# Neighbour attention over 25,000 edges: the node products of blocks 0 to 13 kept in PSUM

## The chip, the cores and the metric

One core of a Trainium2 chip. The time is the device time of one execution in microseconds; of several executions the median is given. A second number, the span, goes from the first to the last instruction of one profiled execution.

## The reference

50,000 nodes with 64 features, 25,000 edges sorted by destination, 10 relations. Each edge's source and destination row is multiplied with its relation's 64x64 matrix, a score comes from both and the edge's features, a softmax over the edges of one destination weighs the source rows, and the sum updates the node. A layer norm over all nodes follows.

```python
proj = jnp.einsum('ni,rio->nro', nfeat, relation_weight)
t_r = proj[src, etype]
h_r = proj[dst, etype]
att = jnp.sum(t_r * jnp.tanh(h_r + efeat), axis=-1)
ex = jnp.exp(att - segment_max(att, dst)[dst])
a = ex / segment_sum(ex, dst)[dst]
h_nb = jax.ops.segment_sum(nfeat[src] * a[:, None], dst, num_segments=n)
out = leaky_relu((nfeat + h_nb) @ res_fc_w.T, 0.01) + leaky_relu(nfeat * h_nb @ res_fc2_w.T, 0.01)
x = _layernorm(x + out, axis=-1)
```

A node without edges has h_nb = 0, so its row needs x and one product alone.

## The kernel before

**Two kinds of work.** The dense part runs over all nodes in 49 tiles of 1,024 rows (128 x 512 numbers): transposes on TensorE into `tr_ps`, a copy to `dT` on ScalarE, a product with `bd_cat` into `y_ps`, relu and sum into `zd`, mean and variance, scaling into `o_t`, store. The edge part runs over 25 blocks of 8 columns of 128 edges (the last block has 4). A partition holds consecutive edges, so a segment's sums run along its columns. GpSimd gathers the source and the destination row of each column with one indirect DMA a column and side into `xsd` (L450, 388 of them; four columns come in single rows over SyncE's queue) and later scatters the finished rows with one indirect DMA a column (L474, 196), which overwrite the dense rows of the nodes with edges. All gathers stand ahead of all scatters in GpSimd's list.

**Steps.** Every engine runs a list in a fixed order, step by step, s from -1 to 28. In step s the edge part projects block s, takes scores, weights and sums of block e = s-1, ends block f = s-2 (node products), centres block l = s-3 and scales an earlier one (`final_out`, from step 5 on). Up to step 15 it also takes the dense tiles D0, D1, D2 = 3s+3, 3s+4, 3s+5 (step 15 has one). For the projection VectorE makes nine masked copies `xm` of the transposed rows (`mask`, L999, a ring of four) and TensorE multiplies each, and one plain copy `xc`, with a relation's matrix (`quad`, ten a step, L558 and L560).

**The pair.** For a block that ends, ScalarE scales the sums into h (`heads`, L779), VectorE makes uw = (h + x, h * x) (`pair`, L1092 and L1093), TensorE transposes it into `tr_ps` in two groups (`pair_turn`, L588), ScalarE copies each to `uwT` (`pair_copy`, L788) and TensorE multiplies with the weights.

- Blocks 0 to 13 (f < LATE = 14): h is in SBUF (`h_t`). Four quarters of the product go one after the other into a half of `s_ps` (`pair_y`, L598) and are copied to `l12` in SBUF (`pair_out`, L793). VectorE takes leaky relu over l12 (`leaky`, L1099), adds its halves (`final_add`, L1104) and x (`final_add_x`, L1109).
- Blocks 14 to 24, when no dense tile is left that uses `y_ps`: h is in `y_ps`. The products with `bd_relu` (0.99 of the weights) go to `y_ps` (L609), the linear part (0.01 of the weights, `bd_lin`) to `tr_ps` (L616). VectorE adds relu of both and the linear part to x straight from PSUM (L1114, L1119, L1125).

Three groups of users share PSUM: `tr_ps` the dense transposes and the pair's, `y_ps` the dense tiles (until step 15), `s_ps` scores and quarters.

**GpSimd's waits.** Ahead of each gather or scatter `pace` may wait for TensorE: a list of marks, made by `pe_marks`, gives TensorE's work in instructions (16 a quad, 16 a dense product, 8 for four transposes), and transfer n waits for the last mark at or below n x 14.6 - 250 (13.64 for a scatter). A gather of block s also waits for the end of block s-13, a scatter for `final_out` of its block. Between the scatters of blocks 20 and 21 GpSimd gathers `es_end`, from which the last node of each partition is mended at the end.

## Time and profile before

| | us |
|---|---|
| median of 3 runs | 761.22 (760.61 to 765.5) |
| the profiled execution | 762.27 |
| its span | 760.5 |
| mean granted clock of TensorE in it | 0.921 of 2.4 GHz |

Durations and starts below come from the profiled execution, counted from the start of its span. The profile lists each engine's busy time, groups of instructions by line, what ended an engine's idle time, and the granted clock by stretch (1.00 is 2.4 GHz, 0.50 is 1.2 GHz). Handing over a DMA is not counted as busy, so GpSimd's time between two indirect DMAs appears as idle time put down to "issue".

### The profile page before, as it was taken

What the parts mean: (1) busy time and instruction counts of PE and PEld (TensorE: products, weight loads), DVE (VectorE), ACT (ScalarE), POOL (GpSimd) and SP (SyncE); (2) the same over time, 40 slices, a digit from 0 to 9 for tenths busy, and PEclk for the clock granted to TensorE, in tenths of its full rate; (3) what the DMA queues carried; (4) which work ended last, traced back from release to release, by engine and by line L of the source; (5) the groups of instructions that cost most, each with busy time, mean ns of one, the idle gap of its engine ahead of it and who ended that gap; (6) DMA issues with size and microseconds to landing.
All of it is one profiled execution on the core that took longest, in us unless ns stands there. A gap on an engine that the chain in (4) does not pass through costs nothing. (4 is left out here: it accounts for less than half of the span.)

```text
span 760.5 us, 13886 instructions
## 1 busy us (share of the span) xinstructions
PE 574.4 (76%) x3948; PEld 313.6 (41%) x3948; DVE 603.9 (79%) x1094; ACT 507.9 (67%) x1457; POOL 575.6 (76%) x594
## 2 busy tenths in 40 slices
PE   1897988888898898798898797898888988650000
PEld 0643454444454454454454453444444444450000
DVE  2589899999999999999999999899888888750010
ACT  0376877779879878878878879656655556770040
POOL 6777777777777777777777777777777777777776
PEclk9999999999999999999999999999999999855555
DMA  4643443343353343354343243321222210000000
GB/s 115 177 123 91 137 152 114 97 151 85 108 165 107 94 155 92 113 151 109 93 155 108 67 124 97 105 67 48 75 75 73 68 48 33 32 25 18 19 18 16
DMA packets 48034, 70.37 MB, mean 93 GB/s; under 512 B 15970, under 2 KB 19486, under 8 KB 47958
## 3 DMA queue, kind: packets, MB, share of 16 engines
q1 hardware_dynamic: 18562, 32.97, 13.8%
q0 software_dynamic: 18752, 17.29, 10.5%
q10 hardware_dynamic: 10644, 19.23, 6.8%
q8 instruction: 32, 0.52, 0.3%
q14 instruction: 44, 0.36, 0.2%
HBM read 45.60 MB, written 25.78 MB: 94 GB/s over the span
## 5 line engine op out<-in xcount | busy, mean ns | idle before, releaser
L450 POOL DMA_INDIRECT xsd<-in_x,ends_i x388 | 380.8, 982 | 119.9 <-issue 107.7
L999 DVE SCALAR_TENSOR_TENSOR xm<-typ,xT_ps 128x1024 f32<-128x1024 f32 (+1 forms) x225 | 264.2, 1184 | 3.0 <-ACT xc L719 2.6
L558 PE MATMUL t_ps<-xm,w_rel 64*64 64x512 f32 (+1 forms) x900 | 241.5, 617 | 13.7 <-DVE xm L999 11.0
L560 PE MATMUL h_ps<-xm,w_rel 64*64 64x512 f32 (+1 forms) x900 | 241.4, 617 | 0.0
L474 POOL DMA_INDIRECT out<-out_r,row_i x196 | 191.7, 978 | 59.7 <-issue 57.0
L578 PE MATMUL y_ps<-bd_cat,dT 128*128 128x256 f32 x392 | 98.4, 395 | 11.3 <-DVE zd L1061 5.4
L743 ACT ACTIVATE o_t<-zd,rstd 128x64 f32<-128x64 f32 x392 | 98.8, 339 | 6.3 <-DVE rstd L1083 6.3
L558 PEld LDWEIGHTS t_ps<-xm,w_rel 64*64 64x64 f32 x900 | 46.9, 133 | 105.2 <-DVE xm L999 76.8
L578 PEld LDWEIGHTS y_ps<-bd_cat,dT 128*128 128x128 f32 x392 | 72.7, 196 | 25.1 <-ACT dT L724 11.0
L588 PE MATMUL tr_ps<-ident,uw 128*128 128x128 f32 x196 | 33.5, 297 | 44.5 <-ACT uwT L788 24.0
L1041 DVE SCALAR_TENSOR_TENSOR es<-es,wd,wx 128x64 f32<-128x64 f32 x196 | 55.2, 282 | 11.2 <-DVE es L1041 0.5
L598 PEld LDWEIGHTS s_ps<-bd_both,uwT 128*128 128x128 f32 x224 | 31.9, 206 | 59.7 <-issue 38.6
L588 PEld LDWEIGHTS tr_ps<-ident,uw 128*128 128x128 f32 x196 | 21.6, 146 | 84.1 <-issue 52.7
L767 ACT ACTIVATE wx<-xsd,wd 128x64 f32<-128x64 f32 x196 | 52.1, 337 | 0.8
L598 PE MATMUL s_ps<-bd_both,uwT 128*128 128x128 f32 x224 | 42.6, 316 | 8.8 <-issue 8.7
L813 ACT ACTIVATE out_r<-zcf,rstd 128x64 f32<-128x64 f32 x196 | 49.1, 333 | 0.0
L1061 DVE TENSOR_TENSOR zd<-rd,y_ps 128x512 f32<-128x512 f32 x49 | 33.3, 680 | 19.1 <-ACT rd L729 17.9
L560 PEld LDWEIGHTS h_ps<-xm,w_rel 64*64 64x64 f32 x900 | 46.9, 133 | 0.0
L761 ACT ACTIVATE wd<-delta 128x16 f32<-128x16 f32 (+1 forms) x25 | 5.4, 216 | 61.6 <-DVE delta L1029 55.6
L806 ACT ACTIVATE sqf<-zcf 128x512 f32<-128x512 f32 (+1 forms) x25 | 15.3, 611 | 43.4 <-DVE zcf L1136 42.2
L736 ACT ACTIVATE sqd<-zd 128x512 f32<-128x512 f32 x49 | 30.9, 630 | 19.8 <-DVE zd L1071 12.0
L713 ACT ACTIVATE g_t<-h_ps 128x512 f32<-128x512 f32 (+1 forms) x25 | 14.7, 588 | 39.1 <-PEq L563 38.3
(161 smaller groups left out, 957.9 us busy)
## 6 DMA issues: line engine op xcount, KB each, us to landing
x_in<-in_x SPq DMA_DIRECT2D x48, 256.0 KB, 2.7
typ<-typ_d SPq DMA_DIRECT2D x24, 512.0 KB
out<-o_t ACTq DMA_DIRECT2D x48, 256.0 KB
xsd<-in_x SPq DMA_DIRECT2D x512, 0.2 KB
xsd<-in_x,ends_i POOLq DMA_INDIRECT x388, 2.7
hist<-es ACTq DMA_DIRECT2D x24, 256.0 KB, 2.7
ea<-in_edge_attr SPq DMA_DIRECT2D x24, 224.0 KB
out<-out_r,row_i POOLq DMA_INDIRECT x196, 2.1
```

The costliest lines, as they stand in the source:

```text
L450: pool.indirect_dma_start(xsd[:, s % RX, j, side, :], None, x[:, :], bass.IndirectOffsetOnAxis(ap=ends_i[:, side, c:c + 1], axis=0),).then ...
L474: pool.indirect_dma_start(out[:, :], bass.IndirectOffsetOnAxis(ap=row_i[:, c:c + 1], axis=0), out_r[:, s % RW, j, :], None, bounds_check=t ...
L558: pe.matmul(t_ps[h * D:(h + 1) * D, 0:n], w[0:D, :], moving[0:D, h * n:(h + 1) * n], start=(at == 0), stop=(at == R - 1), skip_group_check ...
L560: mm = pe.matmul(h_ps[(1 - h) * D:(2 - h) * D, 0:n], w[D:P, :], moving[D:P, (1 - h) * n:(2 - h) * n], start=False, stop=(at == R - 1), ski ...
L578: mm = pe.matmul(y_ps[:, j * 2 * P:(j + 1) * 2 * P], dT[:, d % 2, j * P:(j + 1) * P], bd_cat.rearrange("p k f -> p (k f)"), start=True, st ...
L588: mm = pe.transpose(tr_ps[:, j * P:(j + 1) * P], uw[:, g * QUAD + j, :, :].rearrange("p k f -> p (k f)"), ident[:, :])
L598: mm = pe.matmul(s_ps[:, YQ + j * P:YQ + (j + 1) * P], uwT[:, q // 2, k * P:(k + 1) * P], bd_both[:, :], start=True, stop=True)
L743: ins = act.activation(o_t[:, d % RO, j * D:(j + 1) * D], zd[:, d % RZ, j * D:(j + 1) * D], ACT.Copy, scale=rstd[:, s % 2, d % 3, j:j + 1])
L767: ins = act.activation(wx[:, j, :], xsd[:, e % RX, j, 0, :], ACT.Copy, scale=wd[:, e % 2, 0, j:j + 1])
L813: ins = act.activation(out_r[:, f % RW, j, :], zcf[:, f % 2, j, :], ACT.Copy, scale=rstd[:, s % 2, 3, j:j + 1])
L999: v.scalar_tensor_tensor(xm[:, m % RM, 0:n], typ[:, s % RT, 0:n], float(r), xT_ps[:, 0:n], ALU.is_equal, ALU.mult).then_inc(masked, 1)
L1041: v.scalar_tensor_tensor(es[:, e % RS, j, :], old, wd[:, e % 2, 1, j:j + 1], wx[:, j, :], ALU.mult, ALU.add).then_inc(chain_done, 1)
```

## The change

All blocks take one form. h goes to `tr_ps` (`heads_ps`); the eight products with `bd_relu` go to `y_ps` between the dense tiles D0 and D1 (`pair_y`), the linear part to `s_ps` (`pair_linear`), which the scores use too; VectorE reads h, the products and the linear part from PSUM. `h_t`, `l12`, `pair_out` and `leaky` go. The order moves with it. TensorE: D1's transposes before the products; D2's transposes behind quad 8; quad 9 before D2's product. ScalarE: `tanh` from the step's start to its end; `weights` behind `dense_square`; the pair's copies before and between the `weigh`s, ahead of `final_out`. VectorE: the two relu sums behind mask 6, the linear part behind D1's sum, `final_centre` before mask 6. New waits: `dense_y(D1)` for `relu_second`, `pair_y` for D0's sum, `scores` and `pair_linear` for earlier linear sums, `pair_copy` for all products of the block before. GpSimd's own list and its constants stay; the marks that it waits for are listed in the new order.

```diff
...
@@ -84,7 +83,6 @@
     def quad_count(m):
         return m // RB * R + m % RB + (2 if m % RB >= PLAIN_AT else 1)
-    LATE = (ND - 1) // 3 - 2
     ROW_BLOCKS = [8, 13, 19, 24]
     CHUNK = 16
...
-        def h_late():
-            return y_ps[:, 0:COLS * D].rearrange("p (j f) -> p j f", f=D)
-        def y_late(k, n):
+        heads_ps = tr_ps.rearrange("p (j f) -> p j f", f=D)
+        def y_pair(k, n):
             return y_ps.rearrange("p (j k f) -> p j k f", j=COLS, k=2)[:, 0:n, k, :]
-        def lin_late(n):
-            return tr_ps[:, 0:n * D].rearrange("p (j f) -> p j f", f=D)
+        def y_lin(n):
+            return s_ps[:, 0:n * D].rearrange("p (j f) -> p j f", f=D)
         def turn(n, ring):
             return n // ring + 1
...
@@ -285,24 +275,24 @@
                     mark(att_done, e + 1, 2 * cols(e))
                 multiplied(0)
                 quads(0, 4)
-                if quarters > 0:
+                if pairs:
                     mark(tr_in, TR_PAIR[f, 0] + 1, 8)
                 quads(4, 5)
-                if quarters > 2:
+                if pairs > 1:
                     mark(tr_in, TR_PAIR[f, 1] + 1, 8)
                 quads(5, 6)
-                paired(0)
                 turned(1)
+                if pairs:
+                    mark(y12_done, 2 * f + 1, 2 * cols(f))
                 quads(6, 7)
-                paired(1)
                 multiplied(1)
                 quads(7, 8)
-                paired(2)
+                if pairs:
+                    mark(y12_done, 2 * f + 2, 2 * cols(f))
+                quads(8, 9)
                 turned(2)
-                quads(8, 9)
-                paired(3)
+                quads(9, 10)
                 multiplied(2)
...
                 pe.wait_ge(prod_done, e + 1)
-                wait(pe, delta_done, e)
-                if e >= 2:
-                    pe.wait_ge(pf_done, Q_BEFORE[min(e - 1, LATE)])
+                wait(pe, z2_done, e - 1)
                 half = cols(e) // 2
-                b = (e % 2) * COLS
                 for i in range(half):
-                    pe.matmul(s_ps[:, b + 2 * i:b + 2 * i + 2], prod[:, i * P:(i + 1) * P], ones2[:, :],
+                    pe.matmul(s_ps[:, 2 * i:2 * i + 2], prod[:, i * P:(i + 1) * P], ones2[:, :],
                                    start=True, stop=True)
...
@@ -574,6 +561,8 @@
             def dense_y(d):
                 pe.wait_ge(tr_out, TR_DENSE[d] + 1)
                 wait(pe, zadd_done, d)
+                if d % 3 == 1:
+                    wait(pe, z1_done, d // 3 - 2)
                 for j in range(4):
                     mm = pe.matmul(y_ps[:, j * 2 * P:(j + 1) * 2 * P], dT[:, d % 2, j * P:(j + 1) * P],
                                    bd_cat.rearrange("p k f -> p (k f)"), start=True, stop=True)
...
-            def pair_y(f, q):
-                pe.wait_ge(tr_out, TR_PAIR[f, q // 2] + 1)
-                wait(pe, pf_done, Q_BEFORE[f] + q)
-                wait(pe, delta_done, min(f + 2, NS))
-                for j in range(2):
-                    k = (q % 2) * 2 + j
-                    mm = pe.matmul(s_ps[:, YQ + j * P:YQ + (j + 1) * P], uwT[:, q // 2, k * P:(k + 1) * P], bd_both[:, :],
-                                   start=True, stop=True)
-                mm.then_inc(y12_done, 1)
-            def late_y(f, g):
-                pe.wait_ge(tr_out, TR_PAIR[f, g] + 1)
-                pe.wait_ge(uw_done, f + 1)
-                if f > LATE:
-                    pe.wait_ge(z1_done, f)
-                for k in range(QUAD):
-                    j = g * QUAD + k
+            def pair_y(f):
+                pe.wait_ge(tr_out, TR_PAIR[f, groups(f) - 1] + 1)
+                pe.wait_ge(zadd_done, min(ND, 3 * f + 10))
+                wait(pe, z1_done, f)
+                for j in range(cols(f)):
+                    g, k = divmod(j, QUAD)
                     mm = pe.matmul(y_ps[:, j * P:(j + 1) * P], uwT[:, g, k * P:(k + 1) * P], bd_relu[:, :], start=True, stop=True)
                 mm.then_inc(y12_done, 1)
-            def late_linear(f, g):
-                pe.wait_ge(tr_out, TR_PAIR[f, groups(f) - 1] + 1)
-                for k in range(QUAD):
-                    j = g * QUAD + k
-                    mm = pe.matmul(tr_ps[:, j * D:(j + 1) * D], uwT[:, g, k * P:(k + 1) * P], bd_lin[:, :], start=True, stop=True)
+            def pair_linear(f):
+                pe.wait_ge(delta_done, min(f + 2, NS))
+                wait(pe, z2_done, f)
+                for j in range(cols(f)):
+                    g, k = divmod(j, QUAD)
+                    mm = pe.matmul(s_ps[:, j * D:(j + 1) * D], uwT[:, g, k * P:(k + 1) * P], bd_lin[:, :], start=True, stop=True)
                 mm.then_inc(y12_done, 1)
-            def pair_part(f, q):
-                if f < LATE:
-                    pair_y(f, q)
-                elif q < groups(f):
-                    late_y(f, q)
-                else:
-                    late_linear(f, q - groups(f))
...
                 if main:
                     quad(s, 5)
-                if quarters > 0:
-                    pair_part(f, 0)
                 if D1 is not None:
                     dense_turn(D1)
+                if ending:
+                    pair_y(f)
                 if main:
                     quad(s, 6)
-                if quarters > 1:
-                    pair_part(f, 1)
                 if D1 is not None:
                     dense_y(D1)
                 if main:
                     quad(s, 7)
-                if quarters > 2:
-                    pair_part(f, 2)
-                if D2 is not None:
-                    dense_turn(D2)
+                if ending:
+                    pair_linear(f)
                 if main:
                     quad(s, 8)
                 if s == NS:
...
                 if D2 is not None:
+                    dense_turn(D2)
+                if main:
+                    quad(s, 9)
+                if D2 is not None:
                     dense_y(D2)
...
                 act.wait_ge(frec_done, f + 1)
-                wait(act, uw_done, f)
-                if f == LATE:
-                    act.wait_ge(zadd_done, ND)
-                if f > LATE:
-                    act.wait_ge(z1_done, f)
-                h = h_late() if f >= LATE else h_t
+                wait(act, tr_out, TR_PAIR[f, 0])
                 for j in range(g * QUAD, (g + 1) * QUAD):
-                    ins = act.activation(h[:, j, :], es[:, f % RS, j, :], ACT.Copy, scale=rs[:, f % 2, j:j + 1])
+                    ins = act.activation(heads_ps[:, j, :], es[:, f % RS, j, :], ACT.Copy, scale=rs[:, f % 2, j:j + 1])
                 ins.then_inc(h_done, 1)
             def pair_copy(f, g):
                 act.wait_ge(tr_in, TR_PAIR[f, g] + 1)
-                if f > LATE:
-                    act.wait_ge(y12_done, Q_BEFORE[f])
-                elif f > 0:
-                    act.wait_ge(y12_done, min(Q_BEFORE[f - 1] + 2 * g + 2, Q_BEFORE[f]))
+                wait(act, y12_done, 2 * f)
                 act.copy(uwT[:, g, :], tr_ps[:, :]).then_inc(tr_out, 1)
-            def pair_out(f, q):
-                act.wait_ge(y12_done, Q_BEFORE[f] + q + 1)
-                wait(act, z1_done, f)
-                act.copy(l12[:, 2 * q:2 * q + 2, :, :],
-                         s_ps[:, YQ:YQ + 2 * P].rearrange("p (j k f) -> p j k f", j=2, k=2)).then_inc(pf_done, 1)
             def roots(s):
...
                 D0, D1, D2 = (n if n in tiles(s) else None for n in (3 * s + 3, 3 * s + 4, 3 * s + 5))
                 DP = 3 * s + 2 if 3 * s + 2 in tiles(s - 1) else None
-                quarters, done = 2 * groups(f) if 0 <= f < NS else 0, tiles(s - 1)
-                if 0 <= e < NS:
-                    tanh(e)
...
                     store_o(n)
-                if 0 <= s - 2 < NS:
-                    store_hist(s - 2)
-                if 0 <= e < NS:
-                    weights(e)
-                    weigh(e, 0)
+                if ending:
+                    store_hist(f)
                 if DP is not None:
                     dense_square(DP)
+                if on:
+                    weights(e)
+                if ending:
+                    pair_copy(f, 0)
+                if on:
+                    weigh(e, 0)
+                if ending and groups(f) > 1:
+                    pair_copy(f, 1)
+                if on and groups(e) > 1:
+                    weigh(e, 1)
                 if 0 <= o - 1 < NS and s <= NS:
                     final_out(o - 1, s - 1)
-                if quarters > 0:
-                    pair_copy(f, 0)
-                if 0 <= e < NS and groups(e) > 1:
-                    weigh(e, 1)
-                if quarters > 2:
-                    pair_copy(f, 1)
                 if s >= 0:
                     roots(s)
-                if quarters > 0 and f < LATE:
-                    pair_out(f, 0)
                 if D1 is not None:
                     dense_copy(D1)
...
                     final_square(l)
-                if D1 is not None:
-                    dense_relu(D1)
-                if quarters > 2 and f < LATE:
-                    pair_out(f, 2)
+                for n in done[1:2]:
+                    dense_norm(n)
+                for n in done[1:2]:
+                    store_o(n)
                 if D2 is not None:
                     dense_copy(D2)
-                for n in done[1:2]:
-                    dense_norm(n)
-                if quarters > 3 and f < LATE:
-                    pair_out(f, 3)
-                for n in done[1:2]:
-                    store_o(n)
+                if 0 <= s < NS:
+                    tanh(s)
                 if D1 is not None:
...
                     v.wait_ge(tr_in, TR_PAIR[f - 1, groups(f - 1) - 1] + 1)
-                h = h_late() if f >= LATE else h_t
-                v.tensor_tensor(uw[:, 0:n, 0, :], h[:, 0:n, :], xd, ALU.add)
-                v.tensor_tensor(uw[:, 0:n, 1, :], h[:, 0:n, :], xd, ALU.mult).then_inc(uw_done, 1)
-            def leaky(f):
+                v.tensor_tensor(uw[:, 0:n, 0, :], heads_ps[:, 0:n, :], xd, ALU.add)
+                v.tensor_tensor(uw[:, 0:n, 1, :], heads_ps[:, 0:n, :], xd, ALU.mult).then_inc(uw_done, 1)
+            def relu_first(f):
                 n = cols(f)
-                v.wait_ge(pf_done, Q_BEFORE[f + 1])
-                l = l12[:, 0:n, :, :].rearrange("p j k f -> p (j k f)")
-                v.scalar_tensor_tensor(l, l, SLOPE, l, ALU.mult, ALU.max).then_inc(l_done, 1)
-            def final_add(f):
+                wait(v, fsub_done, f)
+                v.wait_ge(y12_done, 2 * f + 1)
+                v.scalar_tensor_tensor(zf[:, 0:n, :], y_pair(0, n), 0.0, xsd[:, f % RX, 0:n, 1, :], ALU.max, ALU.add).then_inc(l_done, 1)
+            def relu_second(f):
                 n = cols(f)
                 v.wait_ge(l_done, f + 1)
-                v.tensor_tensor(zf[:, 0:n, :], l12[:, 0:n, 0, :], l12[:, 0:n, 1, :], ALU.add).then_inc(z1_done, 1)
-            def final_add_x(f):
+                v.scalar_tensor_tensor(zf[:, 0:n, :], y_pair(1, n), 0.0, zf[:, 0:n, :], ALU.max, ALU.add).then_inc(z1_done, 1)
+            def linear_last(f):
                 n = cols(f)
                 v.wait_ge(z1_done, f + 1)
-                v.tensor_tensor(zf[:, 0:n, :], zf[:, 0:n, :], xsd[:, f % RX, 0:n, 1, :], ALU.add).then_inc(z2_done, 1)
-            def late_first(f):
-                n = cols(f)
-                v.wait_ge(y12_done, Q_BEFORE[f] + groups(f))
-                v.scalar_tensor_tensor(zf[:, 0:n, :], y_late(0, n), 0.0, xsd[:, f % RX, 0:n, 1, :], ALU.max, ALU.add).then_inc(l_done, 1)
-            def late_second(f):
-                n = cols(f)
-                v.wait_ge(l_done, f + 1)
-                v.scalar_tensor_tensor(zf[:, 0:n, :], y_late(1, n), 0.0, zf[:, 0:n, :], ALU.max, ALU.add).then_inc(z1_done, 1)
-            def late_third(f):
-                n = cols(f)
-                v.wait_ge(z1_done, f + 1)
-                v.wait_ge(y12_done, Q_BEFORE[f + 1])
-                v.tensor_tensor(zf[:, 0:n, :], zf[:, 0:n, :], lin_late(n), ALU.add).then_inc(z2_done, 1)
+                v.wait_ge(y12_done, 2 * f + 2)
+                v.tensor_tensor(zf[:, 0:n, :], zf[:, 0:n, :], y_lin(n), ALU.add).then_inc(z2_done, 1)
             def final_sum(f):
                 n = cols(f)
...
                 if late:
                     final_sum(l)
+                if late:
+                    final_centre(l)
                 if main:
                     mask(s, 6)
+                if ending:
+                    relu_first(f)
+                if ending:
+                    relu_second(f)
                 if on:
                     sum_one(e, 4)
                     sum_one(e, 5)
...
                 if D0 is not None:
                     dense_centre(D0)
-                if late:
-                    final_centre(l)
...
                 if D1 is not None:
                     dense_add(D1)
+                if ending:
+                    linear_last(f)
                 if D1 is not None:
...
                     inverse(e)
-                if ending and f < LATE:
-                    leaky(f)
-                    final_add(f)
-                if ending and f >= LATE:
-                    late_first(f)
-                    late_second(f)
                 if main:
                     product(s)
-                if ending and f < LATE:
-                    final_add_x(f)
-                if ending and f >= LATE:
-                    late_third(f)
                 if D0 is not None:
                     dense_sum(D0)
...
```

## Rows read from the trace of the kernel before

**Rows 1.** the page's first part: busy time of each engine, its share of the span, instructions

```profile
PE 574.4 (76%) x3948; PEld 313.6 (41%) x3948; DVE 603.9 (79%) x1094; ACT 507.9 (67%) x1457; POOL 575.6 (76%) x594
```

**Rows 2.** the chain that ended last, its last scatter: start, us, what

```profile
754.85 0.97 POOL out L474
```

**Rows 3.** GpSimd's gathers by line: shortest/median/longest ns, first and last start

```profile
L450 POOL DMA_INDIRECT xsd<-in_x,ends_i x388: 938/944/1660, 3.5 to 502.2; - x194
```

**Rows 4.** timeline of VectorE at the end: start, us, what [idle before it, releaser]

```profile
721.17 0.28 DVE L1274 SCALAR_TENSOR_TENSOR before<-es_end,fix,xT_ps 128x64 f32<-128x64 f32 x1 [36.89 <-DMA es_end<-hist,fix_i]
```

**Rows 5.** gathers by stretch (33:88, 88:469, 479:503): busy us, mean ns | idle, releasers

```profile
L450 POOL DMA_INDIRECT xsd<-in_x,ends_i x44 | 42.3, 961 | 14.1 <-issue 12.2 <-PE y_ps L578 0.7 <-PE h_ps L560 0.6
...
L450 POOL DMA_INDIRECT xsd<-in_x,ends_i x296 | 292.1, 987 | 90.3 <-issue 82.4 <-PE h_ps L560 6.4 <-PE s_ps L598 0.9
...
L450 POOL DMA_INDIRECT xsd<-in_x,ends_i x20 | 18.9, 947 | 6.1 <-issue 5.5 <-PE h_ps L560 0.6
```

**Rows 6.** timeline of GpSimd in step 9

```profile
284.10 1.29 POOL L450 DMA_INDIRECT xsd<-in_x,ends_i  x1 [0.30 <-PE h_ps L560]
...
301.97 1.65 POOL L450 DMA_INDIRECT xsd<-in_x,ends_i  x1 [0.31 <-issue]
```

**Rows 7.** timeline of VectorE in step 9

```profile
279.00 1.21 DVE L999 SCALAR_TENSOR_TENSOR xm<-typ,xT_ps 128x1024 f32<-128x1024 f32 x1
...
284.49 0.68 DVE L1093 TENSOR_TENSOR uw<-h_t,xsd 128x512 f32<-128x512 f32 x1
...
301.57 1.23 DVE L1099 SCALAR_TENSOR_TENSOR l<-l 128x1024 f32<-128x1024 f32 x1
302.83 0.69 DVE L1104 TENSOR_TENSOR zf<-l 128x512 f32<-128x512 f32 x1
...
304.48 0.68 DVE L1109 TENSOR_TENSOR zf<-zf,xsd 128x512 f32<-128x512 f32 x1
```

**Rows 8.** timeline of VectorE in a step of the late form

```profile
511.18 0.64 DVE L1114 SCALAR_TENSOR_TENSOR zf<-y_ps,xsd 128x512 f32<-128x512 f32 x1
511.85 0.69 DVE L1119 SCALAR_TENSOR_TENSOR zf<-y_ps,zf 128x512 f32<-128x512 f32 x1
```

**Rows 9.** steps: length; busy of PE, PEld, DVE, ACT, POOL; clock, DMA

```profile
142.80:170.10 27.30, 24.07 (x167) 13.14 (x167) 26.50 (x47) 21.86 (x63) 20.90 (x22) 1.00 0.41 123
...
198.70:227.30 28.60, 25.29 (x168) 13.71 (x169) 26.67 (x46) 24.00 (x72) 21.85 (x22) 0.94 0.42 124
227.30:255.40 28.10, 23.73 (x168) 13.07 (x168) 26.57 (x46) 23.80 (x71) 21.46 (x22) 1.00 0.40 119
```

**Rows 10.** timeline of ScalarE in step 9

```profile
285.80 0.63 ACT L736 ACTIVATE sqd<-zd 128x512 f32<-128x512 f32 x1 [0.49 <-DVE zd L1071]
286.34 2.00 ACT L813 ACTIVATE out_r<-zcf,rstd 128x64 f32<-128x64 f32 x8
...
293.60 0.35 ACT L793 COPY l<-s_ps 128x256 f32<-128x256 f32 x1
293.85 0.59 ACT L724 COPY dT<-tr_ps 128x512 f32<-128x512 f32 x1
...
304.57 1.01 ACT L719 COPY xc<-xT_ps 128x1024 f32<-128x1024 f32 x1 [0.74 <-PEq L522]
```

**Rows 11.** timeline of TensorE in step 9 and in a late step

```profile
288.96 0.96 PE L588 MATMUL tr_ps<-ident,uw 128*128 128x128 f32 x4 [2.06 <-ACT uwT L788]
...
294.75 1.89 PE L578 MATMUL y_ps<-bd_cat,dT 128*128 128x256 f32 x8
...
303.45 1.06 PE L520 MATMUL xT_ps<-ident,xsd 128*128 128x128 f32 x8 [0.30 <-issue]
...
509.29 1.10 PE L616 MATMUL tr_ps<-bd_lin,uwT 128*128 128x64 f32 x8
```

**Rows 12.** timeline of TensorE: last matmuls of block 5's second quad

```profile
168.02 0.59 PE L558 MATMUL t_ps<-xm,w_rel 64*64 64x512 f32 x1
```

**Rows 13.** timeline of GpSimd: the gather that asks for it

```profile
177.42 0.94 POOL L450 DMA_INDIRECT xsd<-in_x,ends_i  x1 [0.30 <-issue]
```

37 lines of the change are left out of this document (11 added, 26 removed).

## The prediction

> **What bounds the kernel.** I read the engines' sums on the page first. No engine looks full: VectorE 79%, TensorE and GpSimd 76%, ScalarE 67% [rows 1]. The chain that ended last says more: it consists of GpSimd's scatters alone, one after the other, 0.97 us each, the last at 754.85 [rows 2]. So I read GpSimd's own instructions next. The 388 gathers start at 3.5 us and have a median of 944 ns [rows 3]; the idle time before one is 90.3/296 = 0.305 us and is almost all put down to "issue", the handing over of a DMA [rows 5]. The 584 transfers at 0.944 or 0.97 plus 0.305 make 388 x 1.249 + 196 x 1.275 = 735 of the 751 us from the first start to the last: they stand back to back, and the 16 us left are a few at the start and gathers longer than the median. GpSimd's 76% is a full engine. At the end compute waits for it, too: VectorE stood still for 36.89 us before L1274 until GpSimd's gather of es_end had landed [rows 4]. The kernel ends when GpSimd has issued its list, provided compute never makes it wait. What the change does to VectorE, ScalarE and TensorE counts only through two doors: whether a gather gets longer or shorter, and whether the waits of `pace` or `fmul_done` begin to hold GpSimd.
>
> **First door: lengthened gathers.** The median is 944 ns, the mean is not. From 88 to 469 us there are 296 gathers with a mean of 987; from 33 to 88, before any block ends, 961; from 479 on 947 [rows 5]. The timeline of one step (9) shows where it comes from. The gather at 284.10 took 1.29 us and ended at 285.39; VectorE ran the two instructions of `pair` (uw from h_t and xsd, all in SBUF) to 285.17. The gather at 301.97 took 1.65 us and ended at 303.62; VectorE ran L1099 and L1104 (l12 and zf, all in SBUF) to 303.52. Neighbouring gathers have 0.94 [rows 6, 7]. Such a pair of long gathers recurs in nearly every step that ends one of blocks 0 to 13. In the late steps, where the same work reads PSUM (L1114, L1119, L1125), the gathers stay near 947 [rows 5, 8]. The change gives blocks 0 to 13 exactly the late form: h, both products and the linear part are read from PSUM, so each of these VectorE instructions keeps one SBUF input. What the gain is: at least 987 - 961 = 26 ns, at most 987 - 947 = 40 ns a gather, over 296 gathers 7.7 to 11.8 us. I take the middle, 9.7, because the dense tiles' L1071 (two SBUF inputs, three a step) stays and is in the 961, while the late steps lack it.
>
> The Trainium skill, "SBUF — State Buffer", section "Who interferes with whom", has this mechanism: a VectorE instruction with two SBUF inputs contends with a GpSimd instruction that reads SBUF, and one with at most one such input does not. It also infers that `tensor_tensor` does not hold up descriptor generation, which would speak against the gain (761 by that); the ends of the two gathers above, 0.10 to 0.22 us after the VectorE instruction, disagree.
>
> **VectorE.** Removed a block: L1099 (1.23), L1104 (0.69), L1109 (0.68), 2.60 us. Added: 0.64 + 0.69 and, for L1125's sum of the same 128 x 512, 0.68 again, 2.01 [rows 7, 8]. That is 0.6 us less in a step; a step without final_out takes 27.30 with VectorE busy for 26.50 [rows 9]. **ScalarE** loses four `pair_out` copies (0.36 each, about 0.25 from start to start: L793 at 293.60, L724 at 293.85), 1.0 to 1.4 us [rows 10]. **TensorE** gets more: eight bd_relu products cost what eight bd_both cost, and the eight bd_lin ones are new. The late steps show 1.10 for four, so 2.2 us a step [rows 11]. None of these sets the end, so none is added to the time; they decide the length c of a compute step.
>
> **Second door: pace.** `pace` asks, before gather n, that TensorE has passed a mark of n x 14.6 - 250 in its list. A full dense step weighs 328 in it (24+16+16+48+160+16+32+16; the changed list gives 328 as well), so GpSimd takes 328/14.6 = 22.47 gathers a step. Before, one took (292.1+90.3)/296 = 1.292 us, 29.0 a step, against compute's 28.1 to 28.6 [rows 5, 9]. Gather 134 (the first is 0), the 135th, starts at 177.42 and asks for 1,706, that is block 5's second quad, done at 168.6: TensorE leads by 8.8 us there [rows 12, 13]. After the change a gather takes 1.292 - 9.7/296 = 1.259 us, so a step of GpSimd is 28.3 us. The lead at step 5 is 8.8, less 83 x 0.033 = 2.7, plus about 1.2 for three compute steps 0.4 shorter: 7.3. Over the ten full steps 5 to 14 GpSimd is held for 10 x (c - 28.3) - 7.3, if that is positive.
>
> **The length of a step.** Count from the step's first mask, T. Before, in step 9 (T = 279.00), ScalarE reached `dense_square` of the last tile at T+6.8, and TensorE stood 2.06 us at the second transpose of the pair for uwT, because final_out (2.0 us) ran before the copy. Table loads and roots ended at T+14.6, the copy dT at T+15.4, and TensorE went on to D1's product with no pause, at T+15.75 [rows 7, 10, 11]. After, the square, both copies, both weighs, final_out and the roots all still stand ahead of that copy; weights and the first weigh (1.3 us) come behind the square instead of before it, a wait of about 0.4 for TensorE's transposes is added, and the first pair_out (0.25) and the 0.18 wait of the second copy go: T+15.4 + 1.3 + 0.4 - 0.4 = T+16.7. TensorE, rid of the 2.06 but a little later at the start, has done pair_y and quad 6 by about T+14.1 and now waits some 2.5 us there, before dense_y(D1). The pause has moved, not gone. From D1's product to the end of the next plain copy took 304.57 + 1.01 - 294.75 = 10.8 before [rows 10, 11]; the linear part adds 2.2 and the two quarters that stood there take 1.1 away: 11.9. So c = 16.7 + 11.9 = 28.6, with the overlap of the next mask 28.5, at full clock. VectorE has 27.3 - 0.6 = 26.7 of work and waits about 0.6 for the first wx, 0.7 for the linear part, 0.4 for tanh: 28.4. Both agree.
>
> The clock is the unknown. Of the ten steps from 170 to 454 six show a granted clock of 0.94 (2.4 GHz, but 1.2 for a part), with TensorE busy for 25.29 instead of 23.73; all came behind pauses of 2.06 us, and the step went from 28.1 to 28.6 [rows 9, 11]. After, what follows the pause sets the step, so a fall costs between 0.5 and 1.56. I take 1.0, six times in ten: c = 29.1. GpSimd is then held for 8 - 7.3 = 0.7 us, say 1.4 for uneven steps. Bounds: c = 28.5 gives none, c = 30.1 gives 10.7.
>
> **Other parts.** New waits: `dense_y(D1)` waits for `relu_second`, which VectorE finishes near T+16.3, just ahead of the copy above; if late by x, quad 7 and everything behind it on TensorE is late by x. `scores` waits for the z2 of two blocks earlier, done a step before. D2's x load is released one or two quads later and has a ring of four tiles. z2 comes earlier, so GpSimd's ring wait only eases. Scatters: compute waits 36.89 us for es_end before its last blocks, so an end that comes 10 us sooner leaves it 27 [rows 4].
>
> **Sum.** The profiled execution took 762.3 us, 760.5 of it the span; its time is 1.1 above the median of the three runs. 762.3 - 9.7 + 1.4 = 754.0 for it, and 1.1 less, 752.9, for the median: 753.0.
>
> **Rivals.** (A) Forecast: gathers shrink, pace holds GpSimd under 2 us: 749.5 to 753.6. Chance 0.46. (B) The gathers shrink, but the pause with its clock fall makes c 29.4 to 30.4: held 4 to 14 us, 755 to 765; at c = 29.7, 758. For it: the lead is only 7.3. Chance 0.30. (C) The gathers don't shrink, since other VectorE instructions with two SBUF inputs (L1071, L1136, L1041) catch them now that their phase is free: 761. Against it: the 961 of the early steps. Chance 0.10. (D) Slower: TensorE becomes the bound. Every step has the fall at full price (28.5 + 1.56) and dense_y(D1) waits 0.7 more for `relu_second`: c = 30.8, held 25 - 7.3 = 17.7, 769. It decides from c = 30.0 on, where held time exceeds the 9.7 gained. Chance 0.14.
>
> **Numbers.** About 1% (7.6 us) is what can be told from no change. Faster by more is A, 0.46; within it B and C, 0.40; slower D, 0.14. The range of eight in ten is 749 to 765; A's own is 749.5 to 753.6.
>
> **What will show it.** The mean gather from 88 to 469 us (987, expected 955), no gather of 1.65 us, idle before gathers beyond 0.31 us put down to TensorE (expected under 2 us in all), wx-to-wx steps near 29, TensorE's pause before L578 instead of L588, and the granted clock there. Wrong would be the prediction above all if that pause grew beyond 3 us, or if gathers lengthen at L1071.

## The result, and the profile after

| | before | after |
|---|---|---|
| median of 22 runs each, us | 761.72 | 766.44 |
| ratio, 95% interval | | 1.005, 1.0038 to 1.0062 |
| the profiled execution: time, span | 762.3, 760.5 | 768.5, 766.7 |
| GpSimd's 388 gathers: busy, idle before | 380.8, 119.9 | 373.6, 130.8 |
| first scatter at | 503.4 | 508.9 |

The change is 0.5% slower, within the 1% that the forecast called no change, and outside its range of 749 to 765. First the sums of the page after, to be held against [rows 1], and its two groups of indirect DMAs (busy us, mean ns | idle before, its main releaser):

```profile
PE 595.8 (78%) x4172; PEld 346.9 (45%) x4172; DVE 602.6 (79%) x1094; ACT 496.3 (65%) x1401; POOL 569.1 (74%) x594
...
L440 POOL DMA_INDIRECT xsd<-in_x,ends_i x388 | 373.6, 963 | 130.8 <-issue 102.0
...
L464 POOL DMA_INDIRECT out<-out_r,row_i x196 | 192.4, 982 | 61.5 <-issue 54.8
```

The gathers did get shorter, by 7.2 us, and the idle time before them grew by 10.9 us, which is no longer all "issue". The rest of the 6.2 us of span is 0.7 in the scatters' own time and 1.8 in the idle time before them. From 88 to 469 us, as [rows 5]:

```profile
L440 POOL DMA_INDIRECT xsd<-in_x,ends_i x293 | 282.5, 964 | 99.3 <-issue 77.3 <-PE h_ps L547 8.6 <-PE y_ps L567 5.6
```

The mean fell from 987 to 964 ns, and TensorE's lines now hold gathers: `pace` has begun to wait. Four steps of the kernel after (3, 4, 8 and 9; length, busy time and count of PE, PEld, DVE, ACT, POOL, granted clock, DMA share), as [rows 9]:

```profile
109.50:138.90 29.40, 25.87 (x175) 15.53 (x175) 26.32 (x47) 20.35 (x59) 22.18 (x24) 0.94 0.41 116
138.90:168.70 29.80, 26.51 (x183) 15.80 (x182) 26.53 (x47) 21.15 (x60) 21.24 (x22) 0.94 0.40 114
...
256.90:285.30 28.40, 24.88 (x182) 15.25 (x182) 26.43 (x46) 23.09 (x68) 21.46 (x22) 1.00 0.41 119
285.30:315.30 30.00, 26.52 (x182) 15.67 (x182) 26.37 (x46) 23.07 (x68) 22.05 (x23) 0.94 0.39 115
```

A step takes 28.4 us with the clock at 2.4 GHz all along and 30.0 where it is at 1.2 GHz for a part; before it took 28.1 and 28.6. Steps 3 and 4 took 27.3 before and now have a fall each. Their pause ahead of D1's product ends with `relu_second` (L1045) and not with the copy, here in step 3:

```profile
124.57 0.69 DVE L1045 SCALAR_TENSOR_TENSOR zf<-y_ps,zf 128x512 f32<-128x512 f32 x1
125.41 3.65 PE L567 MATMUL y_ps<-bd_cat,dT 128*128 128x256 f32 x8 [2.73 <-DVE zf L1045]
```

In step 9 (T = 285.33), the rows round D1's product:

```profile
300.82 0.69 DVE L1045 SCALAR_TENSOR_TENSOR zf<-y_ps,zf 128x512 f32<-128x512 f32 x1
301.28 0.57 ACT L689 COPY dT<-tr_ps 128x512 f32<-128x512 f32 x1
301.90 2.76 PE L567 MATMUL y_ps<-bd_cat,dT 128*128 128x256 f32 x8 [2.76 <-ACT dT L689]
...
306.48 2.00 PE L593 MATMUL s_ps<-bd_lin,uwT 128*128 128x64 f32 x16
308.58 0.69 DVE L1051 TENSOR_TENSOR zf<-zf,s_ps 128x512 f32<-128x512 f32 x1 [1.86 <-PE s_ps L593]
308.75 0.94 POOL L440 DMA_INDIRECT xsd<-in_x,ends_i  x1 [0.53 <-PE s_ps L593]
```

TensorE stands 2.76 us for the copy `dT` of D1. `relu_second` (L1045), its second gate, ended only 0.34 us before the copy did (301.51 and 301.85). The fall of the clock comes behind: D1's product takes 2.76 instead of 1.9 us. `pair_linear` follows late, VectorE waits 1.86 us for it, and so does a gather. One wait at the end is new as well, the first scatter's, for the last dense store. That store is issued at 505.81; before, it was at 489.05, 14 us ahead of the first scatter at 503.42. Now:

```profile
508.90 1.00 POOL L464 DMA_INDIRECT out<-out_r,row_i  x1 [2.08 <-DMA out<-o_t]
```

### The profile page after: what moved, and what is told of

Its sections match the earlier page's. It is cut to its first block and busy times, and to the rows that moved or that the text cites. A ratio compares the mean times of both kernels' runs of the same rounds, so it can differ in the third digit from the quotient of the medians.

```text
span 766.7 us, 14235 instructions
## 1 busy us (share of the span) xinstructions
PE 595.8 (78%) x4172; PEld 346.9 (45%) x4172; DVE 602.6 (79%) x1094; ACT 496.3 (65%) x1401; POOL 569.1 (74%) x594
## 5 line engine op out<-in xcount | busy, mean ns | idle before, releaser
L440 POOL DMA_INDIRECT xsd<-in_x,ends_i x388 | 373.6, 963 | 130.8 <-issue 102.0
L943 DVE SCALAR_TENSOR_TENSOR xm<-typ,xT_ps 128x1024 f32<-128x1024 f32 (+1 forms) x225 | 264.5, 1185 | 7.7 <-ACT xc L684 7.5
L545 PE MATMUL t_ps<-xm,w_rel 64*64 64x512 f32 (+1 forms) x900 | 234.9, 617 | 29.4 <-DVE xm L943 28.8
L567 PE MATMUL y_ps<-bd_cat,dT 128*128 128x256 f32 x392 | 111.1, 433 | 48.5 <-ACT dT L689 35.0
L708 ACT ACTIVATE o_t<-zd,rstd 128x64 f32<-128x64 f32 x392 | 98.5, 335 | 16.3 <-DVE rstd L1025 16.3
L593 PEld LDWEIGHTS s_ps<-bd_lin,uwT 128*128 128x128 f32 x392 | 47.8, 199 | 22.0 <-issue 22.0
L585 PE MATMUL y_ps<-bd_relu,uwT 128*128 128x128 f32 x392 | 51.5, 287 | 1.5 <-ACT uwT L745 1.4
L585 PEld LDWEIGHTS y_ps<-bd_relu,uwT 128*128 128x128 f32 x392 | 48.0, 200 | 10.0 <-ACT uwT L745 10.0
L593 PE MATMUL s_ps<-bd_lin,uwT 128*128 128x64 f32 x392 | 51.1, 286 | 0.0
L739 ACT ACTIVATE tr_ps<-es,rs 128x64 f32<-128x64 f32 x196 | 48.6, 302 | 1.3
L694 ACT ACTIVATE rd<-y_ps 128x512 f32<-128x512 f32 x49 | 28.7, 585 | 25.9 <-PE y_ps L567 25.9
L745 ACT COPY uwT<-tr_ps 128x512 f32<-128x512 f32 x49 | 28.6, 584 | 25.5 <-PE tr_ps L575 24.2
```

Of the source, the lines that this page charges most:

```text
L440: pool.indirect_dma_start(xsd[:, s % RX, j, side, :], None, x[:, :], bass.IndirectOffsetOnAxis(ap=ends_i[:, side, c:c + 1], axis=0),).then ...
L545: pe.matmul(t_ps[h * D:(h + 1) * D, 0:n], w[0:D, :], moving[0:D, h * n:(h + 1) * n], start=(at == 0), stop=(at == R - 1), skip_group_check ...
L567: mm = pe.matmul(y_ps[:, j * 2 * P:(j + 1) * 2 * P], dT[:, d % 2, j * P:(j + 1) * P], bd_cat.rearrange("p k f -> p (k f)"), start=True, st ...
L585: mm = pe.matmul(y_ps[:, j * P:(j + 1) * P], uwT[:, g, k * P:(k + 1) * P], bd_relu[:, :], start=True, stop=True)
L593: mm = pe.matmul(s_ps[:, j * D:(j + 1) * D], uwT[:, g, k * P:(k + 1) * P], bd_lin[:, :], start=True, stop=True)
L708: ins = act.activation(o_t[:, d % RO, j * D:(j + 1) * D], zd[:, d % RZ, j * D:(j + 1) * D], ACT.Copy, scale=rstd[:, s % 2, d % 3, j:j + 1])
```

## The experiments

**Which chip.** The first four runs and the last two were taken where the kernel before takes 762 to 763 us. The others fell where it takes 911 to 927; they are compared only with the kernel before beside them and have a section of their own.

In the expectations, **theory P:** the pause ahead of D1's product, with the fall behind it, gives GpSimd's gain back through `pace`. **Rival V:** VectorE's order of masks and relus sets the step, and the pause only shows it. **Rival L:** the gathers stay long, since other instructions with two SBUF inputs hold them.

### Is it the lead? LEAD 600 in both kernels

```diff
-PACE, LEAD, PACE_OUT = 14.6, 250, 13.64
+PACE, LEAD, PACE_OUT = 14.6, 600, 13.64
```

In the kernel after:

> The changed kernel with LEAD 600 in place of 250, so that pace asks some 24 gathers later; compute is untouched. Theory P: the compute step stays 28.4 to 30, but GpSimd is held later or not at all: 10 to 12 us fewer, 754 to 757, unless another wait of GpSimd comes in the place of pace. Rival C (compute itself ends late, pace only shows it): 764 to 767, with GpSimd's waits now put down to o_stored, z2 or fmul.

766.16 us, 1.0063 [1.0043, 1.0083]. The groups of the page, and the wait ahead of the first scatter in the timeline:

```profile
L440 POOL DMA_INDIRECT xsd<-in_x,ends_i x388 | 371.5, 957 | 119.1 <-issue 108.8
...
505.50 1.00 POOL L464 DMA_INDIRECT out<-out_r,row_i  x1 [12.54 <-DMA out<-o_t]
```

No gather is held any more: 11.7 us of idle time are gone and the gathers are 9.3 us shorter than before. Nothing of it reaches the end. GpSimd arrives sooner and stands 12.54 us for the last store of `o_t`, since the scatters overwrite dense rows. Compute's dense phase is a second wall at 505.5, and `pace` only spreads the same wait over the gathers. So this run's rival C is borne out: the loss isn't a matter of pacing, the dense steps are too long.

In the kernel before:

> The kernel before with LEAD 600. Its gathers have an idle time of 0.305 us whatever they wait for, but for two early waits of 0.3 and 0.4 us. Theory P: 760 to 761.5, no difference. Rival: earlier gathers crowd the DMA queues or meet VectorE elsewhere: over 763 or under 758.

762.7 us, 1.0004 [0.9988, 1.002], idle before gathers 119.1 against 119.9. Before, `pace` held next to nothing.

### Are the gathers held by what the forecast said? h in PSUM alone

The kernel before with h of blocks 0 to 13 in `tr_ps`:

```diff
-                h = h_late() if f >= LATE else h_t
+                h = h_late() if f >= LATE else lin_late(COLS)
```

> The kernel before with one part of the change alone: in blocks 0 to 13 the scaled sums h go to tr_ps, which is free there, in place of h_t in SBUF, so that both instructions of pair keep one SBUF input. Nothing else moves. Theory G (a gather is held until a VectorE instruction with two SBUF inputs ends, and its own end comes 0.82 us later): the gathers held by pair, 10 to 14 of them with 3.3 to 5.4 us in all, go, those held by leaky stay: 756 to 759. Rival N (the lengthening has another cause than the inputs' place): 761 to 762.

761.6 us, 0.9992 [0.9979, 1.0005]: theory G's 756 to 759 didn't come. The gathers' busy time fell by 1.3 us only, 380.8 to 379.5, and that isn't clear of chance (383.1 in the kernel before with LEAD 600). The timeline of the same place in its step 9 says why:

```profile
283.80 0.68 DVE L1094 TENSOR_TENSOR uw<-tr_ps,xsd 128x512 f32<-128x512 f32 x1
284.01 0.94 POOL L450 DMA_INDIRECT xsd<-in_x,ends_i  x1 [0.30 <-issue]
284.40 0.68 DVE L1095 TENSOR_TENSOR uw<-tr_ps,xsd 128x512 f32<-128x512 f32 x1
284.99 0.68 DVE L1073 SCALAR_TENSOR_TENSOR zd<-zsd,zd 128x512 f32<-128x512 f32 x1
285.25 1.24 POOL L450 DMA_INDIRECT xsd<-in_x,ends_i  x1 [0.30 <-issue]
```

`pair` (L1094 and L1095, now with one input in PSUM) holds nothing: the gather that started 0.21 us into it took 0.94. The next one started 0.26 us into `dense_centre` (L1073 here, L1071 in the kernel before), which has both inputs in SBUF, and ended at 286.49, 0.82 us after that instruction did. That is the rule in all traces. In the kernel before, 49 of the 50 gathers that took over 0.964 us ended 0.81 to 0.82 us after the end of a VectorE instruction with two SBUF inputs that was running as they started; in the kernel after 33 of 34 (0.81 to 0.83). The other one is the very first gather in both. So the forecast named the wrong ends. In [rows 6, 7] the gather at 301.97 ended 0.82 after L1099, not 0.10 after L1104, and the one at 284.10 ended 0.82 after the first instruction of `pair`, not 0.22 after L1093:

```profile
283.88 0.68 DVE L1092 TENSOR_TENSOR uw<-h_t,xsd 128x512 f32<-128x512 f32 x1
```

Taking one such instruction away lets the next one catch a gather. In the kernel after it is `dense_centre` (L1013):

```profile
279.91 0.69 DVE L1013 SCALAR_TENSOR_TENSOR zd<-zsd,zd 128x512 f32<-128x512 f32 x1
280.00 1.42 POOL L440 DMA_INDIRECT xsd<-in_x,ends_i  x1 [0.30 <-issue]
```

### The copy first

The kernel after, `dense_copy(D1)` ahead of `final_out` and the roots:

```diff
+                if D1 is not None:
+                    dense_copy(D1)
                 if 0 <= o - 1 < NS and s <= NS:
                     final_out(o - 1, s - 1)
                 if s >= 0:
                     roots(s)
-                if D1 is not None:
-                    dense_copy(D1)
```

> The changed kernel, with ScalarE's copy of D1 moved ahead of final_out and the roots. Theory P (the pause before D1's product makes the compute step long, with its clock falls; pace passes that on to GpSimd): TensorE's pause of 2.8 us before D1's product goes, no granted clock below 1.00 in steps 5 to 14, a step is 28.1 us or less, GpSimd's idle time over 0.305 a gather falls from about 12 to under 3 us: 753 to 757 us. Rival L (pace's list and lead as such hold GpSimd, whatever ScalarE's order): 765 to 768. Rival M (the pause only moves to another place, as it did with the change): steps stay 28.4 to 30, 763 to 768.

776.54 us, 1.0199 [1.0165, 1.0233]: 10 us worse, where theory P wanted a gain. The timeline of its step 9:

```profile
299.73 0.58 ACT L689 COPY dT<-tr_ps 128x512 f32<-128x512 f32 x1
300.21 2.02 ACT L764 ACTIVATE out_r<-zcf,rstd 128x64 f32<-128x64 f32 x8
302.34 0.69 DVE L1062 SCALAR_TENSOR_TENSOR zcf<-zs,zf 128x512 f32<-128x512 f32 x1 [0.58 <-ACT out_r L764]
304.80 0.69 DVE L1045 SCALAR_TENSOR_TENSOR zf<-y_ps,zf 128x512 f32<-128x512 f32 x1
305.63 0.67 PE L567 MATMUL y_ps<-bd_cat,dT 128*128 128x256 f32 x2 [3.14 <-DVE zf L1045]
```

The copy is early and TensorE waits longer, for the other gate: a later `final_out` delays `final_centre`, which waits for its buffer, which delays the relus behind it. The two gates hang together through ScalarE's list, and theory P, which knew one of them, was too small; a pause that only moves is what its rival M had said.

### Runs on the slower chips

There the compute engines show much more idle time put down to issue, and the mean granted clock is 0.82 to 0.87 instead of 0.92. TensorE's waits in the kernel after (its run beside the third doubled `zf`; waited for, us, times, longest):

```profile
PE y_ps L567 <- issue: 56.0, 30, 7.2
PE t_ps L545 <- issue: 27.3, 18, 4.2
PE y_ps L567 <- DVE zf L1045: 25.8, 8, 7.3
```

A dense step takes 34 to 40 us, `pace` holds GpSimd throughout (247.2 us idle before gathers), and compute is the bound of every kernel. What causes it stays open. It needn't belong to the chip: the record gives number 4 to the chip where the kernel before took 912 and, fifty minutes later, to one where it took 763. The durations of single instructions are as elsewhere (a mask 1,185 ns, a gather 962), so what shows in rows is still to be used. Two kernels tried both gates earlier. First `dense_copy(D1)` between `final_out` and the roots, and, on VectorE, both relus ahead of mask 6 (ScalarE's move is shown):

```diff
-                if s >= 0:
-                    roots(s)
                 if D1 is not None:
                     dense_copy(D1)
+                if s >= 0:
+                    roots(s)
```

> The changed kernel with both gates ahead of D1's product opened a little: ScalarE copies D1 right behind final_out, ahead of the roots, and VectorE runs the two relu sums ahead of mask 6. Theory G2 (two gates stand close behind each other, the copy of D1 at T+16.6 and the relu sums at T+16.2, so that moving one alone gains nothing; the first scatter adds a third wall, the last dense store): the pause before D1's product falls from 2.8 to about 1.5 us, steps to 27.5 to 28.4, GpSimd is held for under 4 us: 756 to 760. Rival M (the pause moves on to another place): 763 to 768.

> The kernel after with dense_copy(D1) between final_out and the roots (the table load and roots, 1.3 us, go behind it) and both relus of the pair ahead of mask 6. Each gate of D1's product comes about 1.2 us sooner, none is put behind final_out. Theory P: pause 1.5 us instead of 2.8, at the price of the roots 0.6 us later; falls of the clock become rare; steps near 28, time 756 to 761. Rival V: the pause goes but mask 6 is later by 1.4 us and quad 6, in front of D1's product, waits for it: the pause moves there and time stays 763 to 768.

1.0283 [1.0214, 1.0351] and, on another chip, 1.0257 [1.0177, 1.0337]. Second, the copy ahead of `final_out`, the relus right behind `final_sum`, and `zf` with two buffers (the moves aren't shown):

```diff
-        zf = sb("zf", [P, COLS, D])
+        zf = sb("zf", [P, 2, COLS, D])
```

> The changed kernel with zf in two buffers, so that the relu sums wait neither for final_centre nor, through it, for final_out; they run before it, and D1's copy runs ahead of final_out and the roots. Theory G2: the pause before D1's product is under 1 us, no clock falls in steps 5 to 14, steps of 26.8 to 28, GpSimd back to back and no wait for the last dense store: 753 to 757, below both kernels. Rival M: steps of 28.4 and more, 763 to 768.

> The kernel after with dense_copy(D1) ahead of final_out and the roots, zf with two buffers and the relus right behind final_sum, and pair_linear where the change put it. Both gates of D1's product (the copy and relu_second) come some 1.5 to 2.5 us sooner. Theory P: the pause shrinks below 1.5 us, most falls of the clock go, steps near 27.8, time 753 to 758. Rival V: final_centre, now behind the relus, waits for a late final_out and delays mask 6 and what follows; steps stay at 29 to 30, 764 to 776.

> dense_copy(D1) ahead of final_out, zf with two buffers, relus right behind final_sum, pair_linear in its place, again. On a chip where the kernel before takes about 762: theory P: pause before D1's product under 1.5 us, most falls of the clock gone, 753 to 758; rival V: 764 to 776, since final_centre waits for a later final_out and delays mask 6. On a chip where the kernel before takes over 900: 4% slower than before, as twice already.

1.0415 [1.0323, 1.0508], 1.0419 [1.0352, 1.0486] and 1.0331 [1.0287, 1.0374]. The kernel after as it is, on the chip of the last of these:

> The kernel after, unchanged, for comparison on the same chip. On a chip where the kernel before takes about 762: 764 to 768. On a chip where the kernel before takes over 900, where compute is the bound: theory P says 2.5 to 3.5% slower than before, since the pause and the 2.2 us of pair_linear behind it count in every step there (the same move of pair_linear was worth 20 us between the two kernels with zf doubled); rival V says at most 1% slower.

1.0132 [1.0086, 1.0178], less than the 2.5 to 3.5% that theory P gave. So the doubled `zf` with its order costs 2 points where compute is the bound: TensorE's wait ahead of D1's product does shrink there, from 3.2 to 1.7 us a step (mean of steps 5 to 14), but the one ahead of D2's grows from 1.2 to 2.1. Neither order was run where the kernel before takes 762, so what they would do there isn't shown.

**The dummy instructions.** The kernel before with 32 VectorE instructions of 128 x 512 more in steps 17 to 24, once with two SBUF inputs, once with one:

```diff
+                if 17 <= s < NS:
+                    v.scalar_tensor_tensor(rd[:, 1, :], rd[:, 0, :], 1.0, sqd[:, 0, :], ALU.mult, ALU.add)
```

```diff
+                if 17 <= s < NS:
+                    v.tensor_reduce(zsd[:, :], rd[:, 0, :].rearrange("p (j f) -> p j f", f=D), AX.X, ALU.add)
```

> The kernel before with four more VectorE instructions in each of the steps 17 to 24 (32 in all), 128 x 512, both inputs in SBUF, 0.69 us; they compute nothing that is used. Theory G: each catches a scatter with a chance of 0.69/1.275 and holds it for 0.35 on average: scatters 4 to 7 us longer in all, 765 to 769. Rival (their VectorE time costs, not their inputs): the same time as its twin with one input. Rival N: 761 to 762.

> The twin: the same 32 places, instructions of 0.68 us with one input in SBUF (a sum along the row). Theory G: no scatter is held by them: 761 to 762, since the late steps have time left (21.2 + 2.7 us against GpSimd's 24). Rival (VectorE's time costs): as its twin, above 764.

913.91 and 911.58 us, against 911.86: the time says nothing, since GpSimd isn't the bound there. The timeline does. With two inputs, then with one:

```profile
654.12 0.68 DVE L1198 SCALAR_TENSOR_TENSOR rd<-rd,sqd 128x512 f32<-128x512 f32 x1
654.25 1.40 POOL L474 DMA_INDIRECT out<-out_r,row_i  x1 [1.29 <-PE h_ps L560]
```

```profile
652.73 0.68 DVE L1198 TENSOR_REDUCE zsd<-rd 128x8 f32<-128x512 f32 x1
652.91 0.97 POOL L474 DMA_INDIRECT out<-out_r,row_i  x1 [1.33 <-PE h_ps L560]
```

All six scatters that started 0.13 to 0.40 us into a dummy with two inputs took 1.14 to 1.40 us and ended 0.84 to 0.85 us after the dummy. The thirteen that started 0.13 to 0.51 us into a dummy with one input took 0.97 to 0.98. The two dummies differ in their operation too, but the kernels' own instructions settle that. Over all twenty traces, 465 transfers started 0.10 us or more into a VectorE instruction with two SBUF inputs and 0.20 or more before its end: every one was held. Of 3,750 that started so in one with an input of two in PSUM (the masks, `pair`, the relus, `scalar_tensor_tensor` and `tensor_tensor` alike) none took over 0.03 us more than usual. It is the number of SBUF inputs, not the work.

### pair_linear in the pause

The kernel after with its eight products, ready since `pair_copy`, ahead of `dense_y(D1)`; the mark that `pace` reads moves along:

```diff
+                if ending:
+                    pair_linear(f)
                 if D1 is not None:
                     dense_y(D1)
                 if main:
                     quad(s, 7)
-                if ending:
-                    pair_linear(f)
```

> The kernel after with one move in TensorE's list: pair_linear (eight products, 2.2 us, whose operands have been ready since pair_copy) goes ahead of dense_y(D1), into the pause; the mark that pace reads moves with it. Theory P (the 2.8 us pause before D1's product and what stands behind it set the step, at 28.4 us, or 30.0 with the clock fall that follows): the pause shrinks to about 0.6 us, the falls go, the work behind the copy is 2.2 us less, VectorE's own 26.7 us and its small waits set the step at 27.0 to 27.6; pace no longer holds a gather (idle before gathers 119 to 121 us), the last dense store comes before GpSimd has done its gathers, first scatter 494 to 498, time 751 to 756. Rival V (VectorE's relu_second at T+16.2 and its order of masks set the step, TensorE's pause only shows it): the pause goes but the step stays at 28 or more, time 760 to 766. Rival L (the gathers are held by other two-input instructions so that the list is no shorter): idle 119 but gathers busy 379 or more, time 760.

> pair_linear ahead of dense_y(D1), as before, again. On a chip where the kernel before takes about 762: theory P: steps 27.0 to 27.8 us, no clock falls but at the start, idle before gathers 119 to 122 us, first scatter 494 to 499, 751 to 757. Rival V: steps 28 or more, 760 to 766. On a chip where the kernel before takes over 900: within 1% of it, as in the run before (1.0056).

> pair_linear ahead of dense_y(D1), once more, for a chip where the kernel before takes about 762. Theory P (the pause ahead of D1's product gives GpSimd's gain back): steps 27.0 to 27.8 us, clock falls rare, idle before gathers 119 to 122 us, first scatter 494 to 499, 751 to 757. Rival V (VectorE's order sets the step): steps 28 or more, 760 to 766. Where the kernel before takes over 900: 0.5 to 1% slower than it, as in the two runs before.

In the three slower runs 1.0056 [1.0015, 1.0097], 1.01 [1.0045, 1.0154] and 1.0113 [1.0038, 1.0188]; beside the kernel after on one of them (924.5 and 925.0) no difference. Together with the doubled `zf`:

> The same move of pair_linear, together with dense_copy(D1) ahead of final_out and the roots, zf with two buffers, and the relus of the pair right behind final_sum. Theory P: no pause of TensorE over 0.5 us is left in the step; VectorE sets it, at 27.0 to 27.6, as in the run with the move alone, so the time is the same as there within 2 us: 751 to 756. If it is 4 us or more better than the move alone, the 0.6 us left in that pause counted each step. Rival V: slower than the move alone, since ScalarE's norm and final_out come later and final_centre waits for them, steps 28 or more, 760 to 768.

1.0152 [1.0067, 1.0237], 20 us less than the doubled `zf` alone on that chip (943.5, 963.4). Then where the kernel before takes 763.2:

> pair_linear ahead of dense_y(D1), for a chip where the kernel before takes about 762. Theory P (the pause ahead of D1's product gives GpSimd's gain back): steps 27.0 to 27.8 us, clock falls rare, idle before gathers 119 to 122 us, first scatter 494 to 499, 751 to 757. A part of the pause may reappear ahead of D2's product, as it did on the slower chips (2.7 us); if it is over 1.5 us here, steps stay above 28 and the time is 758 to 764. Rival V (VectorE's order sets the step): steps 28 or more with no pause of TensorE over 1.5 us, 760 to 766.

763.54 us, 1.0004 [0.9987, 1.0021]: the loss is gone, the gain isn't there. The timeline of its step 9 (T = 280.54):

```profile
297.11 1.99 PE L567 MATMUL y_ps<-bd_cat,dT 128*128 128x256 f32 x8 [0.83 <-ACT dT L689]
...
301.64 2.01 ACT L708 ACTIVATE o_t<-zd,rstd 128x64 f32<-128x64 f32 x8
...
304.11 0.59 ACT L689 COPY dT<-tr_ps 128x512 f32<-128x512 f32 x1 [0.47 <-ACT o_t L708]
304.75 2.97 PE L567 MATMUL y_ps<-bd_cat,dT 128*128 128x256 f32 x8 [2.16 <-ACT dT L689]
```

The pause ahead of D1's product shrank from 2.76 to 0.83, as theory P has it, and 2.16 us appeared ahead of D2's, with the fall of the clock behind it. D2's transposes ended at 301.57, and the copy waits 2.5 us behind a `dense_norm` that it doesn't need. A step is 28.2 or 29.9, as in the kernel after. TensorE's pause isn't the cause of the long step, it is the sum of slack that ScalarE's order leaves it: **theory S**, the step is a ring through ScalarE's list, in which each copy `dT` comes late.

### Both copies

The run before this with one move more, on ScalarE:

```diff
+                if D2 is not None:
+                    dense_copy(D2)
                 for n in done[1:2]:
                     dense_norm(n)
                 for n in done[1:2]:
                     store_o(n)
-                if D2 is not None:
-                    dense_copy(D2)
```

> The kernel after with pair_linear ahead of dense_y(D1), and on ScalarE dense_copy(D2) ahead of the dense_norm and store in front of it, which it doesn't need. Theory S (the step is a ring through ScalarE's list: each of the two copies dT comes late behind work that it doesn't need, and TensorE waits at whichever product comes next): the 2.2 us ahead of D2's product go, no fall of the clock in steps 5 to 14, steps 27.0 to 27.6 us, set by VectorE's 26.7 of work; idle before gathers 118 to 121 us, first scatter 494 to 498, time 752 to 756. Rival V (VectorE's order sets the step): the pauses go, steps 28.0 or more, 760 to 764. If the pause moves once more, to the turn of the next block or to its edges, steps 28 to 29, 759 to 764.

751.4 us, 0.9872 [0.9844, 0.99]: faster than the kernel before by 1.3% (five executions), just below theory S's 752 to 756. Its gathers on the page, a full step, and the same place in the timeline of step 9 (T = 271.48):

```profile
L440 POOL DMA_INDIRECT xsd<-in_x,ends_i x388 | 370.2, 954 | 119.1 <-issue 110.1
...
298.90:326.20 27.30, 25.07 (x181) 15.07 (x181) 26.06 (x46) 22.44 (x68) 20.59 (x23) 1.00 0.43 124
...
287.46 1.99 PE L567 MATMUL y_ps<-bd_cat,dT 128*128 128x256 f32 x8 [0.87 <-ACT dT L689]
...
292.16 0.57 ACT L689 COPY dT<-tr_ps 128x512 f32<-128x512 f32 x1
292.63 2.02 ACT L708 ACTIVATE o_t<-zd,rstd 128x64 f32<-128x64 f32 x8
293.21 1.97 PE L567 MATMUL y_ps<-bd_cat,dT 128*128 128x256 f32 x8 [0.27 <-issue]
```

Nothing is left to wait for ahead of D2's product. Nine of the ten steps 5 to 14 take 27.4 to 27.7 us, one 28.8 (the only one with a fall of the clock), VectorE is busy for 26.1 of them, `pace` holds no gather, the first scatter starts at 492.0 without a wait for the last store, and the span is 11.2 us shorter than before: the 10.6 of the gathers, and 0.8 less idle time before them. Rival V's step of 28 or more is refuted; what is left above VectorE's 26.1 is 1.3 us. The move of D2's copy without that of `pair_linear` wasn't run, so how much of the gain each of them brings isn't shown.

## Why the prediction was wrong

**What held.** GpSimd's list bounds the kernel before, and from the first scatter on the kernel after too. The step after was foretold place by place: copy of D1 done at T+16.7 (measured 16.52), a pause of 2.5 us ahead of D1's product (2.76), 28.5 us at full clock (28.4), 1.56 more with a fall (1.6), `relu_second` just ahead of the copy (by 0.34 us).

**First door, 9.7 us.** 7.2 in the kernel after, 9.3 with no gather held (LEAD 600), 10.6 in the fastest version. The size was right for gathers that run free. The reason was half right: two SBUF inputs are it, but each neighbour of that kind holds a gather, `dense_centre` too. That is rival C's mechanism; in the kernel after 2.5 of the 9.7 us were missing, not all of them as C had it. (Each of these sums is from one trace; the kernel before itself has 380.8 us of gathers in one and, with LEAD 600, 383.1 in another.)

The Trainium skill, "SBUF — State Buffer", section "Who interferes with whom", infers that `tensor_tensor` doesn't hold up descriptor generation. For these indirect DMAs the traces disagree: the gather at 284.10 took 1.29 us and ended 0.82 us after L1092, a `tensor_tensor` with both inputs in SBUF.

**Second door, 1.4 us: the steps that failed.** Two terms of "held = 10 x (c - 28.3) - 7.3" were mis-sized.

- *c.* The price of a fall was taken as 1.0 "six times in ten", from the bounds 0.5 and 1.56. The upper bound was the true one, since what follows the pause sets the step: c was 29.35 (462.18 less 168.66 over ten), not 29.1. That is 2.5 us.
- *The lead.* Steps 2 to 4 were taken to be 0.4 shorter each. They have no `final_out` that delays the copy, which is done at T+14.0 and T+14.6 in steps 3 and 4, but `relu_second` is done only at T+15.8 and T+16.3, and it alone stops TensorE for 2.73 and 2.57 us, with a fall behind each; steps 3 and 4 took 29.4 and 29.8 instead of 27.3. Step 5 began 3.5 us later than before instead of 1.2 sooner, so the lead was 8.8 - 2.7 - 3.5 = 2.6. That is 4.7 us, the largest error. The text had named this gate ("if late by x") and priced it at nothing in its sum.
- With both put right, the formula gives 10 x (29.35 - 28.3) - 2.6 = 7.9. Measured were 10.9 more than before: gather by gather, 1.8 in step 4, 8.2 in steps 5 to 14 and 0.8 at 502 to 506, behind the ten steps. The formula stands for the first two, 10.0 together; where the 2.1 between them come from stays open.

**What was overlooked: the second wall.** The forecast took compute's slack from the 36.89 us at the very end [rows 4]. The first scatter asks compute for its last dense store long before that. With LEAD 600 GpSimd came there at 492.96 and waited 12.54 us, until 505.5. With c and the lead as forecast this wait would have ended 2.5 + 4.7 us sooner, at 498.3, while the forecast has the first scatter at 503.4 - 9.7 + 1.4 = 495.1. So this omission alone costs about 3 us (an estimate from those rows). A slack read at the end of the list doesn't hold for a wait in its middle.

**The range.** Rival B (pause and clock make c 29.4 to 30.4, 755 to 765) is the mechanism that came true; with the lead of 2.6 in place of 7.3 its 755 to 765 is 760 to 770, which holds 766.4 (the c measured, 29.35, is at its lower edge). It had 0.30 and belonged on top: the pause, the fall behind it and the price stood in the text.

## What to carry to other kernels

Where a full engine is let forward by the progress of another, a change must be priced on both, from the first step on, and against every wait in the list that names the other engine, not the last one alone. A pause that moves from one product to the next when its cause is removed belongs to a third engine's order: look in its list for work that stands ahead of what is waited for and isn't needed by it. Here that move and one of a ready product into TensorE's pause together turned a loss of 0.5% into a gain of 1.3%.
